# The recurrent layer's units: square blocks in place of masked products, and finish sums left in PSUM

## What is computed

```python
G = jnp.einsum('bclhn,bcshn->bclsh', C_c, B_c)
M = G * L.transpose(0, 2, 3, 4, 1)            # L = exp(segment sums): decay from token s to token l, s <= l
Y_diag = jnp.einsum('bclhn,...', M, x_c)      # y[l] = sum over s <= l of G[l,s] * decay(s,l,head) * dt[s] * x[s]
states = ...                                  # state carried from chunk to chunk, decayed per head
Y_off = jnp.einsum('bclhn,bchpn->bclhp', C_c, states) * state_decay_out
y = (Y_diag + Y_off) + D * x
y = y * silu(gate);  y = y * rsqrt(mean(y**2) + EPS) * norm_w;  return y @ out_proj_w.T
```

## Time and profile before

| | |
|---|---|
| time, median of 3 | 1039.83 us (1039.57 to 1041.65) |
| profiled execution: its own time | 1041.49 us |
| profiled execution: span from first to last instruction | 1039.5 us |
| recurrent units, first L1826 to last | about 750 to 847 us of the span |
| busy share of the whole span | PE 83%, DVE 57%, POOL 47%, ACT 38% |

### The profile page before, as it was taken

The page is one execution under the profiler, slowest core; times in us unless marked ns, Lnnn a source line. Parts: engine busy times, 40 slices in busy tenths (PEclk is TensorE's granted clock), DMA queues, the critical chain, the costliest instruction groups (busy, mean ns, idle before and its releaser), DMA issues.

```text
span 1039.5 us, 21523 instructions
## 1 busy us (share of the span) xinstructions
PE 857.8 (83%) x7798; PEld 556.2 (54%) x7799; DVE 596.7 (57%) x1105; ACT 396.5 (38%) x955; POOL 492.4 (47%) x538
## 2 busy tenths in 40 slices
PE   3099976787778679998589999969689978999995
PEld 2046642332323335664389999633434444799994
DVE  5623336688796242334535655648389845655655
ACT  6322223145557242224234444356401125344441
POOL 2228868048888331213235454223588733455531
PEclk9999988998978889998879999999899988999997
DMA  8313443235656810002946665330000001766644
GB/s 293 108 42 113 124 128 121 108 94 184 187 174 213 320 59 14 31 21 88 412 163 244 240 221 203 97 137 1 0 0 1 1 1 45 275 221 244 244 167 137
DMA packets 47752, 142.25 MB, mean 137 GB/s; under 512 B 10577, under 2 KB 23714, under 8 KB 41154
## 3 DMA queue, kind: packets, MB, share of 16 engines
q0 software_dynamic: 19280, 93.40, 26.7%
q1 hardware_dynamic: 22366, 40.92, 11.0%
q10 hardware_dynamic: 6036, 6.95, 2.0%
HBM read 106.11 MB, written 35.16 MB: 136 GB/s over the span
## 4 chain that ended last, share of the span: by engine, by line
PE 51%; POOL 13%; DMA 12%; DVE 11%; issue 7%; ACT 5%; SPq 1%; POOLq 0%; ACTq 0%; DVEq 0%
PE psum L563 15%; PE psum L536 12%; PE psum L522 8%; PE psum L1826 4%; POOL mem L1538 4%; POOL mem L1536 3%; DMA mem<-w2l_dram 2%; DMA stage<-in_w 2%; POOL mem L246 2%; PE psum L509 1%; PE psum L1853 1%; PE psum L114 1%; DVE mem L1449 1%; DVE mem L315 1%; DVE psum L2033 1%
## 5 line engine op out<-in xcount | busy, mean ns | idle before, releaser
L563 PE MATMUL psum<-mem 128*128 x1536 | 178.9, 273 | 3.7 <-DVE mem L801 2.5
L563 PEld LDWEIGHTS psum<-mem 128*128 128x128 f16 x1536 | 146.3, 98 | 23.9 <-issue 4.7
L912 POOL DMA_INDIRECT y_dram<-mem x64 | 63.4, 991 | 150.4 <-DVE mem L817 147.6
L536 PE MATMUL psum<-mem 128*128 128x128 f16 x2208 | 132.4, 220 | 0.0
L536 PEld LDWEIGHTS psum<-mem 128*128 128x128 f16 x2208 | 128.6, 99 | 0.7
L653 ACT ACTIVATE mem<-psum,mem 128x128 f32<-128x128 f32 x368 | 105.1, 369 | 55.1 <-PE psum L536 53.6
L907 POOL DMA_INDIRECT mem<-xn_dram,mem x64 | 65.8, 1029 | 113.8 <-PE psum L509 85.9
L1403 ACT ACTIVATE mem<-psum 128x512 f32<-128x512 f32 (+1 forms) x160 | 79.9, 552 | 77.0 <-PE psum L1299 50.8
L522 PE MATMUL psum<-mem 128*128 x432 | 102.7, 397 | 0.7 <-issue 0.7
L1449 DVE TENSOR_REDUCE mem<-psum 128x2 f32<-128x1024 f32 (+2 forms) x96 | 87.6, 949 | 20.4 <-PE psum L1273 12.2
L114 PE MATMUL psum<-ones 128*128 128x512 f16 x326 | 92.3, 413 | 0.6 <-issue 0.6
(11 more groups left out here) (250 smaller groups left out, 1481.9 us busy)
## 6 DMA issues: line engine op xcount, KB each, us to landing
stage<-in_w POOLq DMA_DIRECT2D x20, 480.0 KB, 5.1
stage<-in_w POOLq DMA_DIRECT2D x16, 512.0 KB, 3.9
w_rows<-mem SPq DMA_DIRECT2D x4, 2048.0 KB, 21.0
w2h_dram<-mem POOLq DMA_DIRECT2D x20, 240.0 KB, 2.9
w2l_dram<-mem POOLq DMA_DIRECT2D x20, 240.0 KB, 4.4
xn_dram<-mem ACTq DMA_DIRECT2D x32, 128.0 KB, 1.7
mem<-w2h_dram SPq DMA_DIRECT2D x2, 2048.0 KB, 13.2
mem<-w2l_dram SPq DMA_DIRECT2D x2, 2048.0 KB, 19.1
```

The costliest lines, as they stand in the source:

```text
L536: ins = eng.matmul(c.bank(2 * p + j // half)[:, j % half * P:(j % half + 1) * P], mats[q][:, l, k, j * P:(j + 1) * P], x[:, p, k, :], star ...
L563: ins = eng.matmul(c.bank(6)[:, 0:D], a[:, 0 if gated else p, q * half + j, :], w[:, at], start=(i == 0), stop=(i == 3 * CF - 1))
L912: eng.indirect_dma_start(c.y_dram[:, :], bass.IndirectOffsetOnAxis(ap=yidx[:, b:b + 1], axis=0), yo[:, b % 2, :], None).then_inc(s_ys[b % ...
```

## The change

The levels k = 6 and k = 5 no longer use masks. At level 6 the left half is tokens 0 to 63 and the right half 64 to 127, so `unit` multiplies the 64x64 block `G[0:64, t, 64:128]` with `xw[0:64]` and adds to partitions 64 to 127 of the accumulator. At level 5 there are two groups, and two products of a 32x32 block for each tile: rows 0 to 31 into partitions 32 to 63, rows 64 to 95 into partitions 96 to 127. Their width stays 512. POOL doesn't make `gm` for these units (u0, u1, u4, u6, u11, u13, u18, u20). The five finer levels stay as they are.

The finish sum is written back to the accumulator in PSUM instead of `y`, and the gate multiply reads it there. `cs` of a later pair therefore waits for the multiply (`s_y`) and no longer for the sum (`s_ya`).

```diff
+WHOLE = 5
@@ mixer_stage
-    s_gm = n("gm", NU)
+    MASKED = [u[1] < WHOLE for u in UNITS]
+    s_gm = n("gm", sum(MASKED))
@@ pe: cs
             if t >= 4:
-                eng.wait_ge(*s_ya(t - 3))
+                eng.wait_ge(*s_y(t - 3))
@@ pe: unit
-            eng.wait_ge(*s_gm(i + 1))
+            if MASKED[i]:
+                eng.wait_ge(*s_gm(sum(MASKED[:i + 1])))
...
             for j in range(2):
-                ins = eng.matmul(acc(2 * p + j), gm[:, i % RING, j, :], xw[:, i % RING, j, :], start=False, stop=True, skip_group_check=True)
+                t = 2 * p + j
+                if MASKED[i]:
+                    ins = eng.matmul(acc(t), gm[:, i % RING, j, :], xw[:, i % RING, j, :], start=False, stop=True, skip_group_check=True)
+                    continue
+                half = 1 << k
+                for b in range(0, P, 2 * half):
+                    left, right = slice(b, b + half), slice(b + half, b + 2 * half)
+                    ins = eng.matmul(acc(t)[right, :], G[left, t, right], xw[left, i % RING, j, :], start=False, stop=True,
+                                     skip_group_check=True)
@@ dve: finish
-            eng.tensor_tensor(y[:, t % 2, :], acc(t), y0[:, :], ALU.add).then_inc(s_ya.sem, 1)
+            eng.tensor_tensor(acc(t), acc(t), y0[:, :], ALU.add).then_inc(s_ya.sem, 1)
...
-            eng.tensor_tensor(y[:, t % 2, :], y[:, t % 2, :], sg[:, t % 2, :], ALU.mult).then_inc(s_y.sem, 1)
+            eng.tensor_tensor(y[:, t % 2, :], acc(t), sg[:, t % 2, :], ALU.mult).then_inc(s_y.sem, 1)
@@ pool: decayed
-            eng.tensor_tensor(gm[:, slot, :, :], G[:, t:t + 2, :], gmask[:, k, :].unsqueeze(1).to_broadcast([P, 2, P]), ALU.mult)\
-                .then_inc(s_gm.sem, 1)
+            if MASKED[i]:
+                eng.tensor_tensor(gm[:, slot, :, :], G[:, t:t + 2, :], gmask[:, k, :].unsqueeze(1).to_broadcast([P, 2, P]), ALU.mult)\
+                    .then_inc(s_gm.sem, 1)
```

## The result

Over 20 executions of each, the changed kernel takes 1044.57 us (median) and the kernel before 1041.11; the ratio is 1.0031 with a 95% interval of 1.0019 to 1.0043. The forecast was 1037.0, faster, with a range of 1034.3 to 1041.6; the time lies above it. The profiled execution of after took 1042.64 us, span 1040.7, against 1041.49 and 1039.5 of before. It is one of the shorter executions of after, so it shows only 1.2 of the 3.5 us by which the medians differ.

A forecast was written before the change was run, and what follows sets the result against it. No engine bounds all of the recurrent layer: PE and DVE take turns, then DVE, later PE bounds. Terms -0.7 -0.1 -1.2 -0.9 +0.6 = -2.3 us gave 1037.5 from the median, 1036.3 with one clock gain; 1037.0 taken, range 1034.3 to 1041.6.

The forecast's parts named there:

- The finish part: At the pairs' ends, sum in PSUM and shorter gate multiply: 0.1 us for pairs 0 and 1, 1.2 pair 2, 0.9 pair 3.
- The wait of `cs`: At later pairs' `cs`, waiting for the multiply costs 0; without cover, 0.7 us each at two places.
- Blocks overlap: In level-5 units, the two blocks of a tile run at once on PE: no cost, bounds 0 and 1.7 us a unit.
- rival A: Level-5 blocks run one after another on PE, 3.4 us a unit; 3.1 us slower, 1042.9; chance 0.1.
- Changing the division: Entering or leaving block form on PE costs 0.1 us a change; six on the path, 0.6 us, bounds 0 and 1.6.
- Fewer clashes: From 765 to 776 us, DVE's SBUF multiplies wait less often for POOL operations once masks go: 0.7 us gained, bounds 0 and 2.7.
- The clock: Shorter PE idle times before u25 and at the layer's end restore full clock: gains of 1.6 and 1.2 us.
- rival B: Small blocks keep PE's clock down around u1 and u6, 1.6 us each fall; 1039.9, or 1042 with three or more; chance 0.2.

The follow-up runs named there:

- small_awake: Kernel before with every keep-awake product of the whole program made 64x64 in place of 128x128, recurrent units untouched; ratio to before 1.0291.
- finish_awake: Kernel before plus in-place PSUM sum, gate multiply from PSUM, later `cs` wait and full-array extra products around the first units; 0.9942, repeated 0.9970.
- awake: Changed kernel plus full 128x128 products on ones while PE waits for `base` in the first units; ratio to before 0.9961, repeated 0.9931.
- finish_only: Kernel before with only the in-place PSUM sum, gate multiply from PSUM and later `cs` wait, all masks kept; ratio to before 0.9967.
- awake_small: Changed kernel plus 64x64 extra products, equally many and wide, where PE waits in the first units; ratio to before 0.9989, repeated 0.9962.
- blocks_only: Changed kernel with the old finish sum, multiply and `cs` wait, so only the level 6 and 5 blocks; ratio to before 1.0047.

## Why the prediction was wrong, step by step

- *The finish part*, forecast at 2.2 us (0.1, 1.2 and 0.9): 111.21 - 109.30 = 1.9 us at full clock (small_awake and finish_awake). At the pair's end the distance fell by 3.69 - 2.55 = 1.1 us, at the layer's end PE's wait from 1.19 to 0.29 us. In place, the sum takes 0.70 us, inside the bounds. Right.
- *The wait of `cs`*, forecast at 0: no stall at `cs` in after; PE's gap in front of the first unit of the third pair stays what `base` makes it. Right.
- *Blocks overlap*, forecast at no cost: 1.90 us at eight records. Right, and rival A is out. The rule of the Trainium skill, TensorEngine Tiling (Array Packing), Gotcha 1: PSUM Pressure, by which A would have come true, does not hold for these shapes: the records of rows 0 to 31 and of rows 64 to 95 start within 0.01 us of each other (771.50 us) and write one bank, in different partitions.
- *Changing the division*, forecast at 0.6 us: at 768.7 us of after a full product starts 0.52 us behind the last block's record in place of 0.43, 0.1 a change. Right as a price; on the path all block units together cost about 0.3 us at full clock (see awake), so 0.6 was on the high side.
- *Fewer clashes*, forecast at 0.7 us: not there, or not through the masks. L2032, DVE's multiply of x, takes 1015 ns in the mean where it took 1018:

```profile
L2117 POOL TENSOR_TENSOR mem<-mem 128x512 f32<-128x512 f32 x28 | 35.8, 1281 | 1.2 <-PE psum L1831 1.2
...
L2032 DVE TENSOR_TENSOR mem<-mem 128x512 f32<-128x512 f32 x28 | 28.3, 1015 | 0.0
```

  POOL starts its other multiply (L2117) earlier, meets DVE as often, and pays itself: 1281 ns for 1214. In the stretch for which it was counted, from the fifth to the eleventh `base`, after does take 14.5 us for 15.3; but finish_only, which has all its masks, takes 14.6. So what shortens it is where the operations fall, and the bound of 0 was the right value for the masks.
- *The clock*, forecast as a gain of up to 2.8 us from shorter idle times, of which 0.5 was taken: that part came in the profiled execution (u25 at 1.96 us, and the layer's end 1.2 us shorter than the wait alone explains). But it is the smaller part. The step that failed is the one that priced the blocks at nothing ("I take no cost"): it asked only how long PE streams, and put what they do to the clock into rival B, with chance 0.2 and 1.6 us a fall. B is what happened. Its price was too low as well: it counted a fall as one unit at half speed, as in the earlier trace rows, where full products followed. Where blocks follow, one fall lasted 13.6 us and cost 5.1 us until the fifth `base`.
- Against the forecast's own sum: finish -1.9, clashes 0, and clock and blocks together, by the medians of the paired runs, from 0.9967 to 1.0031, about +6.6 us where +0.1 (0.6 for the division less 0.5 for the clock) had been taken.

The row that should have moved the chances was there: from 285 to 295 us PE was busy 9.1 of 10 us with products of part of the array and stayed at 0.50. It was read, and given a chance of 0.2. The units around u0 had held 1.00 before the change, with PE busy only 11.5 of 15 us, but they had held it with full products. The row doesn't settle it by itself, since the stretch at 300 us shown above has the same kinds of product at 1.00; it was a reason to try the shapes apart before pricing them at nothing.

What stays open: how much each size of block counts, and what makes products on part of the array hold the clock in one stretch and lose it in another. Quarter-array products in awake_small helped more than expected, and no run here tells the share of the array from the number of row or column groups. Nor was it tried to give the blocks' saving to POOL in a correct kernel with full products.

## What to carry to other kernels

Cutting a product to the block that is not zero saves next to nothing on TensorE while its width stays (1.90 for 1.97 us), and it can cost the clock: where TensorE takes turns with another engine, a full product, zeros and all, did more here to keep it at 2.4 GHz. Judge a product also by how much of the array works, not by its busy time alone, and ask of each stretch with gaps whether its products bring the clock back after a fall. And give a VectorE operation one input from PSUM where GpSimd works beside it: 1.44 us became 0.69.

## What the runs showed of the hardware

- Keep-awake products of 64x64 in place of 128x128, 326 records in both, of the same width, lowered the granted clock of the whole program from 0.934 to 0.886 in the profiled executions, and the kernel was 2.9% slower.
- Two float32 32x32 blocks in different row and column groups of the array, writing one PSUM bank, run side by side: 1.91 us for eight records of 512 columns, 1.90 for four of 64x64. This is the diagonal case that neither of the earlier trace rows had.
- Square blocks in eight of 28 units brought the granted clock of the whole program from a median of 0.933 to 0.9265 (blocks_only beside before, 12 and 35 executions) and cost 0.5% of the time; at full clock they cost about 0.3 us.
- An operation taken from POOL didn't make VectorE's SBUF multiplies any shorter (1015 ns for 1018); the wait for each other moved to POOL's side.
